# Expert tiles in two groups, each with its own plan, and the last units' chain inside the tile loops

## The chip, the cores and the metric

One core of a Trainium2 chip runs the whole program. The metric is the time of one execution on the device in microseconds (us). The engines are PE (matrix products), DVE (vector), ACT (activations), POOL (general purpose) and SP (which only issues transfers here); each runs its own instruction stream in order and waits for the others by semaphores. All data are float32, except for some masks.

## The reference

The input x is 2 x 2048 tokens of 128 features. Two layers follow one another:

```
h = norm(x) * gamma + beta;  u, z = in_proj(h)
u = silu(causal_conv4(u) + b);  dt, Bm, Cm = x_proj(u)
delta = softplus(dt_proj(dt) + b)
state = exp(delta * A) * state + delta * Bm * u      # per channel (256) and n (16), along the tokens
y = (sum_n(state * Cm) + u * D) * silu(z)
x = layernorm(x + out_proj(y) + x)

scores = softmax(x @ Wg + bg)                        # 8 experts
p, e = top_k(scores, 2)
eo[i] = gelu(x @ W1[i] + b1[i]) @ W2[i] + b2[i]      # 128 -> 512 -> 128
x = layernorm(x + p[0] * eo[e[0]] + p[1] * eo[e[1]])
```

## The kernel before

**Units and hosts.** The tokens are cut into 8 units of 512, u % 2 being the batch row. The state recurrence is a scan along the tokens: `host(j)` on each engine is the loop over unit j's 32 scans (8 quads Q of 4 scans, slot g). DVE multiplies the inflow of a quad (L1365) and runs the four scans (L1382), ACT makes the decays, PE spreads delta and adds the states up (L807), and POOL multiplies the scanned states by C in two operations per quad (`times_c`, L553, "slot"). Between them stand the front of unit j+2 and the back of units j-1 and j-2: output projection (L821), residual (L1396), norm, transpose (L830), logits (L837), the two best experts (`best_two`, `one_hots`, L1424, L1430), ranks (`ranks`: a count on PE, L851 and L853, and an addition on DVE), and places.

**Lists.** Each token goes to two experts. `run` holds the next free row of each expert's region in the DRAM tensor `xs`; `place` turns ranks into row numbers; POOL's `list_rows` (L596) writes 128 rows with an indirect transfer, 8 of them per unit, 64 in all. Behind each expert's last row SP writes 128 filler rows (`tail`, L453).

**The plan.** When all units are ranked, 14 dependent DVE steps (L1513 to L1528) turn the counts into tables: for tile n, up to MAXT = 8192 / 128 + 7 = 71, which expert (`etab`) and which rows (`rtab`). The semaphore `s_plan` counts the steps.

**The tile loops.** Tile n is 128 rows of one expert. SP loads W1 of its expert (L459, ring of 4) and its rows (L465, ring of 8, three ahead). In iteration n PE transposes tile n (`x_T`, L981), makes the hidden product of tile n-1 (L988) and the output product of tile n-2 (L996). DVE copies tile n's transpose (`x_evac`, L1533), works out the row facts of tile n-1 (L1539 to L1547), and finishes tile n-2 (`finish_tile`: bias L1553, probability L1557, row L1560). ACT makes the GELU (L1266). POOL scatters the finished tile into `results` (`scatter`, L673). The end adds the two results of each token and norms them.

**Order around the change.** After `host(7)` each engine first runs the back of units 6 and 7 and only then its tile loop. It is written out by hand: POOL lists unit 6's eight groups of rows, then unit 7's, and nothing of the tile loops starts before `s_plan` is 14 and all 64 listings have landed.

Of the kernel before, what the change touches and what calls it, by code (L numbers as in the profile page):

```python
# [12 lines left out]
P = 128  # L13
# [3 lines left out]
T = 512  # L17
# [11 lines left out]
MAXT = 2 * NTOK // P + E - 1  # L29
ROOM = NTOK // P  # L30
REGION = ROOM + 1
ROWS = 2 * NTOK + 2 * E * P
WIDE = 132

K_PARTS = {"base": E, "thresholds": ROOM, "numbers": MAXT, "lane": E, "one8": E, "idc": TT, "spare": 2 * E, "fold": 4 * 32}
# [37 lines left out]
def mamba_moe(nc, consts, bcsel, du_d, xs, results, x, ln_gamma, ln_beta, in_proj_w, conv_w, conv_b, x_proj_w,  # L73
              dt_proj_w, dt_proj_b, A_log, Dskip, out_proj_w, Wg, bg, W1, b1, W2, b2, out):
    with ExitStack() as ctx:
# [44 lines left out]
        base, thresholds, numbers, lane = const("base"), const("thresholds"), const("numbers"), const("lane")  # L120
# [77 lines left out]
        past = du[:].rearrange("p h t -> p (h t)")[:, 0:MAXT * E].rearrange("p (j e) -> p j e", e=E)  # L198
        pastc = delta[0][:].rearrange("p h t -> p (h t)")[:, 0:MAXT * E].rearrange("p (j e) -> p j e", e=E)
# [20 lines left out]
        tail = sb("tail", [P, E], U32)  # L220
# [18 lines left out]
        xT_bank, h_bank, o_bank = bank[0:2], bank[2:4], bank[5:7]  # L239
# [115 lines left out]
        def _(sp):  # L355
# [67 lines left out]
            def host(j):  # L423
# [15 lines left out]
                if j == 1:  # L439
                    sp.wait_ge(s_idle, 4)  # L440
                    sp.dma_start(xs[bass.ds(E * REGION * P, E * P), :].rearrange("(a p) w -> p a w", p=P), fillb[:])\
                        .then_inc(s_fill, 16)
# [8 lines left out]
            for e in range(E):  # L451
                r = index(tail[0:1, e:e + 1], mybir.EngineType.SP, (E * REGION - 1) * P)
                sp.dma_start(xs[bass.ds(r, P), :], fills[:, e, :]).then_inc(s_tail, 16)  # L453
            sp.wait_ge(s_plan, 14)
# [6 lines left out]
            def load_tile(n):  # L461
                r = index(rtab[0:1, n:n + 1], mybir.EngineType.SP, E * REGION + E - 1)
# [6 lines left out]
            sp.wait_ge(s_fill, 16)  # L469
            sp.wait_ge(s_tail, 16 * E)  # L470
            for b in range(B):
                sp.wait_ge(s_scat[b], 128 * (UNITS // 2))
# [1165 lines left out]
```

## Time and profile before

| | us |
|---|---|
| median of 3 timed runs | 786.08 (785.85 to 788.13) |
| profiled execution, whole | 791.61 |
| its span, first to last instruction | 789.9 |
| busy: PE, DVE, ACT, POOL | 592.4, 670.4, 428.5, 562.2 |

The profile is one execution. Times in it are microseconds from the start of the span. An entry of the timeline is a start, a duration, the engine, the line of the kernel, the operation, what it writes and reads, and in brackets how long the engine was idle before it and what it waited for.

### The profile page before, as it was taken

Reading aid. Unit: us, or ns where it says so; the run is one execution under the profiler, and the core shown is the slowest. Engines: PE = TensorE matmul, PEld = TensorE weight load, DVE = VectorE, ACT = ScalarE, POOL = GpSimd, SP = SyncE. Lnnn points to the kernel's source line nnn. Section 1 sums busy time; section 2 is a strip of 40 time slices with the busy share of each in tenths; the row PEclk is TensorE's granted clock in tenths of the full one; section 3 lists DMA queues with packets and bytes.
Section 4 is the critical chain, followed back from the end, with each engine's and each line's share of the span. In section 5 each row is a group of like instructions: output and inputs, shape, how many; then the busy total and the mean of one; then the engine's idle time right before and its main releaser. Section 6 shows DMA issues by size and latency. Waiting matters only on the chain. (4 is left out here: it accounts for less than half of the span.)

```text
span 789.9 us, 11864 instructions
## 1 busy us (share of the span) xinstructions
PE 592.4 (75%) x3055; PEld 290.2 (37%) x3071; DVE 670.4 (85%) x1349; ACT 428.5 (54%) x886; POOL 562.2 (71%) x538
## 2 busy tenths in 40 slices
PE   9768788887887888788788674676440999998920
PEld 4322222222322222222222121211130899998910
DVE  4287999999999999999998999999823688887855
ACT  3858586577467476657746554334110565555515
POOL 3345877776899799889879788878865356665634
PEclk9899999999999999999999788878755999999975
DMA  3095476566579568647556654864003677776644
GB/s 93 17 224 133 101 172 154 120 160 161 133 163 258 130 160 191 141 119 186 136 132 152 144 124 104 200 158 109 28 28 102 169 201 215 209 211 176 194 167 169
DMA packets 51169, 117.34 MB, mean 149 GB/s; under 512 B 8816, under 2 KB 25008, under 8 KB 43040
## 3 DMA queue, kind: packets, MB, share of 16 engines
q1 hardware_dynamic: 45344, 107.20, 55.7%
q0 software_dynamic: 4320, 8.99, 3.5%
q8 instruction: 26, 0.43, 0.2%
q10 hardware_dynamic: 1440, 0.40, 0.2%
q14 instruction: 39, 0.32, 0.1%
HBM read 100.21 MB, written 16.35 MB: 148 GB/s over the span
## 5 line engine op out<-in xcount | busy, mean ns | idle before, releaser
L553 POOL TENSOR_TENSOR hc<-hs,Crep 128x1024 f32<-128x1024 f32 x128 | 301.0, 2357 | 96.1 <-DVE hs L1382 85.8
L1382 DVE TENSOR_TENSOR_SCAN hs<-bank,state,flow 128x512 f32<-128x512 f32 x256 | 312.9, 1267 | 17.8 <-ACT bank L1125 11.6
L1125 ACT ACTIVATE bank<-bank,negA 128x512 f32<-128x512 f32 x256 | 164.1, 659 | 186.2 <-PE bank L798 182.6
L798 PE MATMUL bank<-delta,sel 64*128 64x512 f32 x512 | 156.7, 691 | 96.6 <-DVE hs L1382 96.2
L1365 DVE TENSOR_TENSOR flow<-flow,bank 128x2048 f32<-128x2048 f32 x63 | 142.9, 2268 | 0.0
L1266 ACT ACTIVATE flow<-bank,b1T 128x128 f32<-128x128 f32 x284 | 80.8, 369 | 57.1 <-PE bank L988 28.7
L798 PEld LDWEIGHTS bank<-delta,sel 64*128 64x128 f32 x512 | 41.8, 198 | 188.7 <-DVE hs L1382 163.6
L673 POOL DMA_INDIRECT results<-flow,idn x71 | 69.8, 983 | 33.1 <-issue 31.3
L807 PE MATMUL bank<-hc,kc 128*32 128x512 f32 x512 | 73.2, 647 | 7.8 <-POOL hc L553 7.8
L996 PE MATMUL bank<-w_sb,flow 128*128 x568 | 75.5, 276 | 4.5 <-ACT flow L1266 3.3
L988 PE MATMUL bank<-flow 128*128 128x128 f32 x568 | 76.8, 279 | 0.0
L596 POOL DMA_INDIRECT xs<-xn,pos x64 | 63.8, 998 | 16.0 <-issue 15.6
L996 PEld LDWEIGHTS bank<-w_sb,flow 128*128 128x128 f32 x568 | 69.1, 192 | 5.3 <-issue 5.2
L988 PEld LDWEIGHTS bank<-flow 128*128 128x128 f32 x568 | 70.2, 195 | 0.6 <-issue 0.2
L735 PE MATMUL bank<-hT,wtapT 128*128 128x512 f32 x128 | 64.4, 618 | 3.5 <-ACT hT L1033 1.5
L843 PE MATMUL bank<-idle_rhs,ones 128*128 128x512 bf16 x115 | 29.9, 380 | 11.4 <-DVE res L1396 6.9
L672 POOL TENSOR_TENSOR carrier<-kc 128x1 f32<-128x1 f32 x71 | 13.1, 185 | 34.5 <-DVE flow L1560 22.3
L1533 DVE COPY flow<-bank 128x128 f32<-128x128 f32 x71 | 20.7, 292 | 19.6 <-PE bank L981 13.0
L735 PEld LDWEIGHTS bank<-hT,wtapT 128*128 128x128 f32 x128 | 21.2, 189 | 40.8 <-issue 33.0
L981 PE MATMUL bank<-ident,xg 128*128 128x128 f32 x71 | 19.9, 281 | 18.2 <-DMA xg<-xs 18.2
L1553 DVE TENSOR_TENSOR flow<-bank,b_rep 128x128 f32<-128x128 f32 x71 | 20.7, 291 | 12.2 <-PE bank L996 5.9
L807 PEld LDWEIGHTS bank<-hc,kc 128*32 128x32 f32 x512 | 10.5, 111 | 53.9 <-issue 38.4
(196 smaller groups left out, 793.3 us busy)
## 6 DMA issues: line engine op xcount, KB each, us to landing
flow<-du_d SPq DMA_DIRECT2D x63, 1024.0 KB
flow<-L_ffn_W SPq DMA_DIRECT2D x71, 256.0 KB
xg<-xs SPq DMA_DIRECT2D x71, 66.0 KB
du_d<-du SPq DMA_DIRECT2D x28, 128.0 KB
xin<-L_attn_x SPq DMA_DIRECT2D x8, 256.0 KB, 3.6
hs<-results SPq DMA_DIRECT2D x8, 256.0 KB, 4.7
out<-hc SPq DMA_DIRECT2D x8, 256.0 KB, 2.0
results<-flow,idn POOLq DMA_INDIRECT x71
```

Of the source, the lines that this page charges most:

```text
L553: nc.gpsimd.tensor_tensor(hc[:, Q % 2, two, :], hs[:, Q % 2, two, :], Crep[u % 3][:].unsqueeze(1).broadcast_to([P, 2, T]), ALU.mult).then_ ...
L596: nc.gpsimd.indirect_dma_start(out=xs, out_offset=bass.IndirectOffsetOnAxis(ap=pos[u % 2][:, n:n + 1], axis=0), in_=xn[u % 2][:, n % TT, : ...
L673: nc.gpsimd.indirect_dma_start(out=results, out_offset=bass.IndirectOffsetOnAxis(ap=idn[:, n % 8:n % 8 + 1], axis=0), in_=ybuf[:, n % 8, : ...
L735: ins = nc.tensor.matmul(o[:], wtapT[:, h, k, :], hT[u % 2][:, k:k + T], start=(k == 0), stop=(k == TAPS - 1))
L798: ins = nc.tensor.matmul(dbank[2 * odd + i][:], sel[rows, odd, q % 4, :], delta[u % 2][rows, q // 4, :])
L807: ins = nc.tensor.matmul(ybank[32 * j:32 * j + 32, :], fold[:, q % 4, :], hc[:, Q % 2, j, :], start=(q % 4 == 0), stop=(q % 4 == 3))
L988: ins = nc.tensor.matmul(h_bank[n % 2][:, P * k:P * k + P], w1r[n % 4][:, P * k:P * k + P], xTs[:, n % 2, :])
L996: ins = nc.tensor.matmul(o_bank[n % 2][:, 0:D], hTs[:, n % 2, k, :], w2_sb[:].rearrange("p e k d -> p (e k d)")[:, bass.ds(e * (HK * D) + ...
L1125: nc.scalar.activation(dbank[G % 4][:], dbank[G % 4][:], ACT.Exp, scale=negA[:, ch:ch + 1]).then_inc(s_ex, 1)
L1266: ins = nc.scalar.activation(hTs[:, n % 2, k, :], h_bank[n % 2][:, P * k:P * k + P], ACT.Gelu, bias=b1T[:, bass.ds(e * HK + k, 1)])
L1365: nc.vector.tensor_tensor(flow[Q % 3][:], flow[Q % 3][:], Brep[:].unsqueeze(1).broadcast_to([P, 4, T]), ALU.mult).then_inc(s_bu, 1)
L1382: nc.vector.tensor_tensor_scan(hs[:, Q % 2, j, :], dbank[G % 4][:], flow[Q % 3][:, j, :], state[:, Q // QUADS % 2, Q % QUADS, j:j + 1], AL ...
```

## The change

The tiles are planned in two groups. Group 0 holds the rows of units 0 to 5, at most 48 + 7 = 55 tiles; group 1 those of units 6 and 7, at most 16 + 7 = 23. MAXT becomes 78. `xs` is twice as large, with a region for each expert and group; the filler rows are written once per group, those of group 1 by ACT. DVE makes the first plan in `host(7)`, one step behind each scan of slots 8 to 22, and a 15th step sets `run` to the regions of group 1. The second plan is one step per tile in iterations 24 to 37. The back of units 6 and 7 is spread over the iterations of the tile loops by a function `back_of_last(n)` on PE, ACT and DVE, and by conditions on n on POOL. Since the loops now run beside that work, their buffers are taken from other tensors, and x_T has one PSUM bank instead of two. SP waits for the rows of group 1 before it loads tile 55.

```diff
-MAXT = 2 * NTOK // P + E - 1
+GROUP_UNITS = (6, 2)
+GROUP_TILES = [2 * T * n // P + E - 1 for n in GROUP_UNITS]
+GROUP_AT = (0, GROUP_TILES[0])
+MAXT = sum(GROUP_TILES)
 ROOM = NTOK // P
 REGION = ROOM + 1
+GROUP_ROWS = (E * REGION + E) * P
+PLANNED = (14, 29)
...
-        w1r = [flow[0][:, r, :] for r in range(4)]
+        w1r = [pre[:, r, :] for r in range(4)]
         xg = sb("xg", [P, 8, WIDE])
-        xTs = flow[1][:, 2, 0:2 * P].rearrange("p (a d) -> p a d", a=2)
-        hTs = flow[1][:, 0:2, :].rearrange("p a (k n) -> p a k n", k=HK)
-        ytmp = flow[1][:, 3, 0:2 * D].rearrange("p (a d) -> p a d", a=2)
-        yprob = flow[1][:, 3, 2 * D:4 * D].rearrange("p (a d) -> p a d", a=2)
-        ybuf = flow[2][:, 0:2, :].rearrange("p a (k d) -> p (a k) d", d=D)
+        xTs = hT[0][:, 0:2 * P].rearrange("p (a d) -> p a d", a=2)
+        hTs = relu[:].rearrange("p a (k n) -> p a k n", k=HK)
+        ytmp = hT[1][:, 0:2 * D].rearrange("p (a d) -> p a d", a=2)
+        yprob = hT[1][:, 2 * D:4 * D].rearrange("p (a d) -> p a d", a=2)
+        ybuf = gated[2][:, 0:2, :].rearrange("p a (k d) -> p (a k) d", d=D)
...
-        xT_bank, h_bank, o_bank = bank[0:2], bank[2:4], bank[5:7]
+        xT_bank, h_bank, o_bank = bank[0], bank[2:4], (bank[1], bank[4])
...
+                    for p in range(2):
+                        sp.dma_start(xs[bass.ds(GROUP_ROWS * p + E * REGION * P, E * P), :]
+                                     .rearrange("(a p) w -> p a w", p=P), fillb[:]).then_inc(s_fill, 16)
...
-            sp.wait_ge(s_plan, 14)
+            sp.wait_ge(s_plan, PLANNED[0])
+            sp.wait_ge(s_silu, UNITS)
...
+            def rows_ready(p):
+                sp.wait_ge(s_plan, PLANNED[p])
+                sp.wait_ge(s_fill, 32)
+                sp.wait_ge(s_tail, 16 * E * (p + 1))
+                for b in range(B):
+                    sp.wait_ge(s_scat[b], 128 * sum(GROUP_UNITS[:p + 1]) // 2)
+
+            rows_ready(0)
...
+                if n + 3 == GROUP_AT[1]:
+                    rows_ready(1)
...
+                    if slot == 15 and not late:
+                        shift_ex(j - 1)
...
+            for n in range(MAXT + 3):
+                if n == 5:
+                    mask_ranks(last - 1)
+                if n == 9:
+                    places(last - 1)
+                    tag_rows(last - 1)
+                if 10 <= n < 10 + 4 * TT and n % 2 == 0:
+                    list_rows(last - 1, (n - 10) // 2)
+                if n == 11:
+                    back_rstd(last)
+                if n == 19:
+                    shift_ex(last)
+                if n == 22:
+                    mask_ranks(last)
+                if n == 25:
+                    places(last)
+                    tag_rows(last)
+                if 26 <= n < 26 + 4 * TT and n % 2 == 0:
+                    list_rows(last, (n - 26) // 2)
+                if n >= 3:
+                    scatter(n - 3)
...
+            def back_of_last(n):
+                if n == 0:
+                    add_states(QUADS * UNITS - 2)
+                if n == 2:
+                    add_states(QUADS * UNITS - 1)
+                if n == 3:
+                    ranks(last - 1)
+                if n == 5:
+                    out_proj(last, (0, 1))
+                if n == 6:
+                    out_proj(last, (2, 3))
+                if n == 14:
+                    xn_T(last)
+                if n == 16:
+                    logits(last)
+                if n == 19:
+                    ranks(last)
...
-                after(pe, e_xe, n - 1)
-                nc.tensor.transpose(xT_bank[n % 2][:, 0:P], xg[:, n % 8, 0:D], ident[:]).then_inc(e_xT, 1)
+                after(pe, e_xe, n)
+                nc.tensor.transpose(xT_bank[:, 0:P], xg[:, n % 8, 0:D], ident[:]).then_inc(e_xT, 1)
...
+            def fill_tail(e):
+                act.wait_ge(s_plan, PLANNED[0] + 2)
+                r = index(tail[1][0:1, e:e + 1], mybir.EngineType.Activation, 2 * GROUP_ROWS - P)
+                act.dma_start(xs[bass.ds(r, P), :], fills[:, e, :]).then_inc(s_tail, 16)
+
+            def back_of_last(n):
+                if n == 13:
+                    xns(last)
+                if n == 15:
+                    xnT_evac(last)
+                if n == 20:
+                    gate_exp(last)
+                if 27 <= n < 27 + E:
+                    fill_tail(n - 27)
...
+            def plan(p, step):
+                at, many = GROUP_AT[p], GROUP_TILES[p]
+                mine = slice(at, at + many)
+                past = past_room[:, 0:many * E].rearrange("p (j e) -> p j e", e=E)
+                pastc = pastc_room[:, 0:many * E].rearrange("p (j e) -> p j e", e=E)
+                cums = cum[:].unsqueeze(1).broadcast_to([P, many, E])
+                after(dve, s_plan, (PLANNED[0] + 1) * p + step)
+                if step == 0:
+                    drained(dve, fill_of((UNITS - 3, UNITS - 1)[p], "ranks"))
+                    ins = nc.vector.tensor_copy(tail[p][:], run[:])
+                if step == 1:
+                    ins = nc.vector.tensor_tensor(count[:], run[:], (base, base2)[p], ALU.subtract)
+                if step == 2:
+                    ins = nc.vector.tensor_tensor(over, count[:].unsqueeze(2).broadcast_to([P, E, ROOM]),
+                                                  thresholds.unsqueeze(1).broadcast_to([P, E, ROOM]), ALU.is_gt)
...
+                if step == 5:
+                    ins = nc.vector.tensor_tensor(past, numbers[:, mine].unsqueeze(2).broadcast_to([P, many, E]), cums,
+                                                  ALU.is_ge)
+                if step == 6:
+                    ins = nc.vector.tensor_tensor(pastc, past, cums, ALU.mult)
...
+                if step == 10:
+                    ins = nc.vector.scalar_tensor_tensor(lrow[:, mine], region[:, mine], float(REGION), within[:, mine],
+                                                         ALU.mult, ALU.add)
...
+                if step == 14:
+                    ins = nc.vector.tensor_copy(run[:], base2)
+                ins.then_inc(s_plan, 1)
...
+                    if 8 <= g < 23 and j == UNITS - 1:
+                        plan(0, g - 8)
...
+            def back_of_last(n):
+                if n == 4:
+                    post(last, 1)
+                if n == 5:
+                    dve.wait_ge(s_plan, PLANNED[0] + 1)
+                    ranks(last - 1)
+                if n == 7:
+                    place(last - 1)
+                if n == 8:
+                    residual(last)
+                if n == 9:
+                    back_stats(last)
+                if n == 17:
+                    best_two(last)
+                if n == 18:
+                    one_hots(last)
+                if n == 20:
+                    ranks(last)
+                if n == 23:
+                    place(last)
+                if 24 <= n < 38:
+                    plan(1, n - 24)
```

In the last host DVE's stream had, from the second unit-5 count on (`rank`, `run`: the ranks; `esum` to `posf`: the places; `hs`: a scan, x4 for four of them; `flow`: an inflow):

```order
L1437 TENSOR_TENSOR rank<-bank,run 128x32
L1440 TENSOR_TENSOR run<-run,bank 128x8
L1382 SCALAR_TENSOR_TENSOR hs<-bank,state,flow 128x512
L1390 TENSOR_TENSOR yg<-bank,gated 128x512
L1365 TENSOR_TENSOR flow<-flow,bank 128x2048
L1382 SCALAR_TENSOR_TENSOR hs<-bank,state,flow 128x512 x4
L1444 TENSOR_REDUCE esum<-ex 128x4
```

The same place on DVE now (`tail`, `count` and `rest` are the plan's first three steps):

```order
L1439 TENSOR_TENSOR yg<-bank,gated 128x512
L1414 TENSOR_TENSOR flow<-flow,bank 128x2048
L1431 SCALAR_TENSOR_TENSOR hs<-bank,state,flow 128x512
L1510 CAST tail<-run 128x8
L1431 SCALAR_TENSOR_TENSOR hs<-bank,state,flow 128x512
L1512 TENSOR_TENSOR count<-run,kc 128x8
L1431 SCALAR_TENSOR_TENSOR hs<-bank,state,flow 128x512
L1514 TENSOR_TENSOR rest<-count,kc 128x256
L1431 SCALAR_TENSOR_TENSOR hs<-bank,state,flow 128x512
L1493 TENSOR_REDUCE esum<-ex 128x4
```

A step of the plan now stands between any two of these scans. On PE the tile loop began, behind the whole chain of units 6 and 7, of which the last two counts stand here (`taken`), with the first two transposes (`ident,xg`):

```order
L853 MATMUL bank<-taken,below 128x8
L851 MATMUL bank<-taken,ones 128x8 x4
L83 TENSOR_LOAD etab
L981 MATMUL bank<-ident,xg 128x128
L83 TENSOR_LOAD etab
L981 MATMUL bank<-ident,xg 128x128
L988 MATMUL bank<-flow 128x128 x4
```

On PE it now begins right behind the host's last addition of states (`hc,kc`), and the two additions that are left stand in iterations 0 and 2:

```order
L825 MATMUL bank<-hc,kc 32x512 x4
L88 TENSOR_LOAD etab
L1010 MATMUL bank<-ident,xg 128x128
L825 MATMUL bank<-hc,kc 32x512 x4
L88 TENSOR_LOAD etab
L1010 MATMUL bank<-ident,xg 128x128
L1017 MATMUL bank<-hT,pre 128x128 x4
L88 TENSOR_LOAD etab
L1010 MATMUL bank<-ident,xg 128x128
L1017 MATMUL bank<-hT,pre 128x128 x4
```

The second addition follows the first tile's output product. On ACT, in iteration 20, the exponential of unit 7's gate now stands between two tiles' GELUs, with a table load on each side:

```order
L1311 ACTIVATE relu<-bank,b1T 128x128
L1178 ACT_TABLE_LOAD
L1178 ACTIVATE ex<-ex 128x32
L88 TENSOR_LOAD etab
L1311 ISA
L1311 ACT_TABLE_LOAD
L1311 ACTIVATE relu<-bank,b1T 128x128
```

Before, that exponential stood ahead of all GELUs, and a single table load between them.

## Rows read from the trace of the kernel before

**Rows 1.** The span in 40 slices, busy tenths of DVE.

```profile
DVE  4287999999999999999998999999823688887855
```

**Rows 2.** The chain of waits in the hole: start, us, what.

```profile
610.57 1.79 DMA xg<-xs
```

**Rows 3.** Timeline: last listings of units 5 and 7, first tile's transpose.

```profile
569.79 0.96 POOL L596 DMA_INDIRECT xs<-xn,pos  x1 [0.30 <-issue]
...
606.88 0.96 POOL L596 DMA_INDIRECT xs<-xn,pos  x1 [0.31 <-issue]
...
611.61 0.47 PE L981 MATMUL bank<-ident,xg 128*128 128x128 f32 x1 [17.90 <-DMA xg<-xs]
```

**Rows 4.** Timeline of one tile in the expert stage, DVE and PE.

```profile
645.18 0.29 DVE L1533 COPY flow<-bank 128x128 f32<-128x128 f32 x1
...
645.67 0.27 PE L981 MATMUL bank<-ident,xg 128*128 128x128 f32 x1
...
645.98 0.29 DVE L1553 TENSOR_TENSOR flow<-bank,b_rep 128x128 f32<-128x128 f32 x1
...
647.06 0.29 DVE L1533 COPY flow<-bank 128x128 f32<-128x128 f32 x1
...
647.57 0.27 PE L981 MATMUL bank<-ident,xg 128*128 128x128 f32 x1
```

**Rows 5.** Timeline, DVE in a tile in which it runs behind.

```profile
724.40 0.29 DVE L1533 COPY flow<-bank 128x128 f32<-128x128 f32 x1 [0.33 <-issue]
...
725.05 0.28 DVE L1553 TENSOR_TENSOR flow<-bank,b_rep 128x128 f32<-128x128 f32 x1
```

**Rows 6.** Timeline of host 7: scans on DVE, multiplications by C on POOL.

```profile
546.14 4.81 DVE L1382 TENSOR_TENSOR_SCAN hs<-bank,state,flow 128x512 f32<-128x512 f32 x4
...
548.67 4.73 POOL L553 TENSOR_TENSOR hc<-hs,Crep 128x1024 f32<-128x1024 f32 x2 [1.58 <-DVE hs L1382]
...
550.87 0.67 DVE L1390 TENSOR_TENSOR yg<-bank,gated 128x512 f32<-128x512 f32 x1
...
556.36 2.34 POOL L553 TENSOR_TENSOR hc<-hs,Crep 128x1024 f32<-128x1024 f32 x1 [0.27 <-DVE hs L1382]
```

**Rows 7.** Busy time by stretch (PE, PEld, DVE, ACT, POOL): chain, plan; a step.

```profile
573.00:594.60 21.60, 9.60 (x64) 7.09 (x64) 5.74 (x35) 2.69 (x7) 12.40 (x26) 0.58 0.08 26
594.60:600.85 6.25, 0.00 (x0) 0.00 (x0) 5.75 (x15) 0.00 (x0) 4.92 (x10) 0.50 0.22 67
...
596.18 0.75 DVE L1520 TENSOR_TENSOR du<-kc,cum 128x568 f32<-128x568 f32 x1
```

**Rows 8.** Timeline: two DVE operations that overlap a POOL multiplication.

```profile
440.59 3.04 DVE L1430 TENSOR_TENSOR taken<-oh 128x32 bf16<-128x32 f32 x1
441.22 2.35 POOL L553 TENSOR_TENSOR hc<-hs,Crep 128x1024 f32<-128x1024 f32 x1
...
506.18 2.36 POOL L553 TENSOR_TENSOR hc<-hs,Crep 128x1024 f32<-128x1024 f32 x1
507.83 0.80 DVE L1424 TENSOR_TENSOR oh<-kc,topi 128x64 f32<-128x64 f32 x1
```

**Rows 9.** Timeline, PE: one addition of states.

```profile
552.06 1.07 PE L807 MATMUL bank<-hc,kc 128*32 128x512 f32 x8
```

**Rows 10.** Timeline, ACT: the table load, and a GELU later in the loop.

```profile
614.70 1.28 ACT L1266 ACT_TABLE_LOAD   x1 [22.24 <-PE bank L988]
615.99 2.17 ACT L1266 ACTIVATE flow<-bank,b1T 128x128 f32<-128x128 f32 x8
...
646.97 1.14 ACT L1266 ACTIVATE flow<-bank,b1T 128x128 f32<-128x128 f32 x4 [0.76 <-issue]
648.57 1.06 PE L996 MATMUL bank<-w_sb,flow 128*128 x8
```

**Rows 11.** Timeline, POOL: scatters that find their tile finished.

```profile
717.40 0.98 POOL L673 DMA_INDIRECT results<-flow,idn  x1 [0.16 <-issue]
...
718.78 0.98 POOL L673 DMA_INDIRECT results<-flow,idn  x1 [0.16 <-issue]
```

More of the change, by code:

```diff
@@ L118, in const @@
             return kc[:, K_AT[name][0]:K_AT[name][1]]
[L120 removed]
+        base, base2, thresholds, numbers, lane = (const(n) for n in ("base", "base2", "thresholds", "numbers", "lane"))
         one8, idc, spare = const("one8"), const("idc"), const("spare")
@@ L219, in mamba_moe @@
         prob = sb("prob", [P, 8])
-        tail = sb("tail", [P, E], U32)
+        tail = [sb(f"tail{p}", [P, E], U32) for p in range(2)]
         fillb = sb("fillb", [P, E, WIDE])
@@ L651, in _ @@
                 host(j)
-            last = UNITS - 1
-            shift_ex(last - 1)
-            mask_ranks(last - 1)
-            places(last - 1)
-            tag_rows(last - 1)
-            for n in range(TT):
-                list_rows(last - 1, n)
-            back_rstd(last)
-            for n in range(TT, 2 * TT):
-                list_rows(last - 1, n)
-            shift_ex(last)
-            mask_ranks(last)
-            places(last)
-            tag_rows(last)
-            for n in range(2 * TT):
-                list_rows(last, n)
             def scatter(n):
@@ L675, in scatter @@
                     in_=ybuf[:, n % 8, :], in_offset=None).then_inc(e_sc[n % 8], 16)
-            for n in range(MAXT):
-                scatter(n)
+            last = UNITS - 1
+            for n in range(MAXT + 3):
[19 more added lines that the diff above has]
+                    scatter(n - 3)
             for u in range(UNITS):
@@ L1450, in place @@
                 nc.vector.reduce_sum(posf[:], masked[:].rearrange("p k t e -> p (k t) e"), AX_X).then_inc(s_pf, 1)
+            def plan(p, step):
[13 more added lines that the diff above has]
+                                                  thresholds.unsqueeze(1).broadcast_to([P, E, ROOM]), ALU.is_gt)
+                if step == 3:
+                    ins = nc.vector.reduce_sum(tiles[:], over, AX_X)
+                if step == 4:
+                    ins = nc.vector.tensor_tensor_scan(cum[:], one8, tiles[:], 0.0, ALU.mult, ALU.add)
+                if step == 5:
[3 more added lines that the diff above has]
+                    ins = nc.vector.tensor_tensor(pastc, past, cums, ALU.mult)
+                if step == 7:
+                    ins = nc.vector.reduce_sum(region[:, mine], past, AX_X)
+                if step == 8:
+                    ins = nc.vector.reduce_max(first[:, mine], pastc, AX_X)
+                if step == 9:
+                    ins = nc.vector.tensor_tensor(within[:, mine], numbers[:, mine], first[:, mine], ALU.subtract)
+                if step == 10:
+                    ins = nc.vector.scalar_tensor_tensor(lrow[:, mine], region[:, mine], float(REGION), within[:, mine],
+                                                         ALU.mult, ALU.add)
+                if step == 11:
+                    ins = nc.vector.tensor_scalar(expert[:, mine], region[:, mine], float(E - 1), None, ALU.min)
+                if step == 12:
+                    ins = nc.vector.tensor_scalar(rtab[:, mine], lrow[:, mine], float(GROUP_ROWS // P * p), None, ALU.add)
+                if step == 13:
+                    ins = nc.vector.tensor_copy(etab[:, mine], expert[:, mine])
+                if step == 14:
+                    ins = nc.vector.tensor_copy(run[:], base2)
+                ins.then_inc(s_plan, 1)
```

84 lines of the change are left out of this document (25 added, 59 removed).

## The prediction

> **What bounds the kernel now.** I read first the span in slices [rows 1]: DVE is at nine tenths until slice 27, falls to 2 and 3 in slices 28 to 30, and is at eight or so from there on. So there are a scan stage that DVE bounds, a hole, and an expert stage. The chain of waits has at the hole's end the wait for a tile's rows, which were just written [rows 2]. The timeline gives its edges, with POOL's listings of rows ahead of that wait [rows 3]: the last listing of unit 5 starts at 569.79, the last one of unit 7 at 606.88, and the first tile's transpose follows that by 4.73 us, at 611.61. In the expert stage PE's transposes come every 1.90 us (645.67, 647.57) and DVE's copies as well (645.18, 647.06) [rows 4]. Both engines are on the path there: PE is never idle, and DVE's whole idle time in a tile is the 0.16 us by which the step from its copy to the bias addition (0.80 in [rows 4]) exceeds that of a tile in which DVE ran behind (0.65, [rows 5]).
>
> The sum is made against the profiled execution (span 789.9, time 791.61). The median of the timed runs is 786.08, so 5.5 lower; I carry a difference over unchanged.
>
> **The start moves forward: -37.1.** The first group needs the rows of units 0 to 5 only. With the same 4.73 us behind the listing at 569.79 its first transpose would start at 574.5 instead of 611.6 [rows 3]. The W1 loads and the fills of the first group stand behind the host's last transfers on SP and are issued before that. The second filler transfer of 528 KB on SP in host 1 has three flow buffers ahead of it as cover, so I take it at nothing; uncovered it would delay a scan quad by a few us once.
>
> **The first plan goes into the last host: +8.8.** DVE gets 15 steps there, one behind each scan from the 9th to the 23rd, and host 7 runs at DVE's pace up to there: POOL waits 1.58 us for a scan at 548.67. From that point to the end of the host POOL is the late one (it waits 0.27 once more, at 556.36) [rows 6], so what DVE loses before 550 shifts the listings one for one. The 14 steps took 5.75 us of DVE time for 71 tiles [rows 7]. Four of them have 568 elements and take 0.75; with 440 they save 0.15 each, and a small copy is added: 5.3. Behind a scan an operation starts some 0.08 before its end (546.14 + 4.81 against 550.87 [rows 6]), which takes off 1.1: **4.2**.
>
> To this come collisions with POOL. At 507.83 a DVE operation on two SBUF operands that takes 0.2 alone lasted 0.80 and ended 0.09 behind POOL's multiplication [rows 8]. POOL's multiplication of 2.35 us starts some 0.1 behind the second scan of four (546.14 + 2.4, 548.67 [rows 6]). So a step behind the third scan, 1.2 us later, finds it running for another 1.15. Steps 2, 6, 10 and 14 stand there: 4 x 1.15 = **4.6**. Bounds: 4.2 if none is held, 13.6 for the rival below. I take 8.8, since each overlap in [rows 8] cost DVE the whole remainder.
>
> The Trainium skill (SBUF — State Buffer, Who interferes with whom) says that of a DVE operation with two SBUF inputs and a GpSimd operation that reads SBUF the one that issues first keeps the shared port for its whole length. By that rule the steps behind a second scan, which DVE issues just ahead of POOL, would be free, as the sum has them. A row disagrees: at 440.59 DVE was 0.63 ahead of POOL's multiplication and still ended behind it, after 3.04 us [rows 8]. There POOL had the operation queued right behind a listing; in host 7 it waits idle for the scan, so I keep these steps free and leave the row to a rival.
>
> **Seven tiles more: +13.3.** 55 + 23 = 78 tiles instead of 71, each 1.90: 7 x 1.90 [rows 4].
>
> **The chain on PE: +6.2.** It stands behind the tiles' products on an engine without idle time, so it counts in full. Two additions of states at 1.07 [rows 9] are 2.1. Output projection (two groups of 8 matmul records), logits (one) and the transpose (half a group) go at the loop's pace for such a group, (1.90 - 0.1) / 2 = 0.9: 3.2. The two rank products are some 0.45 each: 0.9. Bounds: 5.0 if the first addition falls into the wait for the first copy, 7.5 if the early ones run at the slow clock. That x_T has one bank instead of two adds nothing that the following product would not wait for anyway: both wait for the same copy.
>
> **The chain on DVE: +6.0.** Its operations of the last two units took 5.74 us in the hole [rows 7], at nine tiles of the loop. Each tile hides 0.16, and in tile 5 PE has work of its own: 5.7 - 1.4 - 0.3, and 0.5 for waits between dependent steps, makes 4.5. The second plan has 184 elements where there were 568, 3.7 us in all; over 14 tiles 2.2 of it is hidden: 1.5. Upper bound, nothing hidden: 9.6; lower bound 4.5.
>
> **On ACT: +1.6.** The exponential in tile 20 stands between GELUs: two table loads of 1.28 and 0.23. ACT is idle 0.76 in a tile, and PE needs its result only 0.46 later [rows 10]: 2.8 - 1.2 = 1.6. The normalization of 1.65 in tile 13 exceeds this by 0.4, which PE's transpose in tile 14 covers. The eight tail transfers from ACT fit in the idle 0.76; without that cover some 0.3 each, 2.4 in all.
>
> The Trainium skill (ScalarE: Activation LUTs, What ACT_TABLE_LOAD costs) gives a switch 1.28 us and 1.38 more for a drain. By that page the sum would be 2.8 higher. The trace does not agree: the load at 614.70 ends at 615.98 and the GELU starts at 615.99 [rows 10].
>
> **On POOL: +1.0.** From tile 5 to 42 it gets 16 listings at 1.27 (0.96 and 0.31 of issue, 606.88) and some 7 us of small work: 27. A scatter that finds its tile done takes 1.38 instead of 1.90 (717.40 to 718.78) [rows 3, 11], so 37 tiles give 19 back, and eight buffers allow a lag of about five tiles (9.5) more. It just fits; 1.0 is for collisions. Queued behind POOL's waits for ranks and places are the scatters, and DVE's row indices wait for scatters eight tiles back: 0 to 6.
>
> **Sum:** -37.1 + 8.8 + 13.3 + 6.2 + 6.0 + 1.6 + 1.0 = -0.2. Span 789.7, median **785.9**. The hole is really emptied, and nearly all of it is paid back in three places.
>
> **Rivals.** (B) *The plan steps aren't held by POOL.* For it: most additions of the logarithm in earlier hosts ran beside a free port. Against it: [rows 8]. Then -4.6: 781.3.
> (C) *Slower: DVE loses the port also behind the second scan.* For it: 440.59 [rows 8]. Steps 1, 5, 9 and 13 then wait 2.35 each and those behind them go free: 9.4 - 4.6 = +4.8, 790.7. It decides as soon as two of the four are held.
> (D) *DVE's idle time in the loop can't be used*, since PE takes up its copy almost at once; every operation of the chain counts in full: +3.6, 789.5. For it: only 0.22 lie between the copy's end (647.35) and PE's next transpose (647.57) [rows 4].
> (E) *The change doesn't do what it says: the second group isn't ready.* SP asks for it at tile 52, which it reaches when PE is at tile 49; POOL's last listing stands at its tile 40. With a lag over eight tiles the loop stops there: +10 or more, 796. Against it: a lag of five tiles already stops DVE.
>
> **How the numbers follow.** Forecast 0.43, B 0.27, C 0.14, D 0.11, E 0.05. What a measurement tells from no change is 0.3%, 2.4 us: below 783.7, above 788.4. The forecast's own range is 781.5 to 791 by the bounds of its terms, of which 0.12 lies below and 0.10 above that band; B gives 0.24 to faster, C, D and E 0.26 to slower. Faster 0.36, same 0.28, slower 0.36. The likeliest single case is a difference too small to see. The range 779 to 794 takes in B, C and D and leaves out E and the sums of several bounds.
>
> **What would show it.** The first tile's transpose at 583 (574.5 + 8.8); at 578 B is right, at 588 C. The 15 plan steps in host 7: those behind third scans at 1.3 us and more, the others at 0.2 to 0.6. A tile period of 1.90 outside tiles 0 to 38, and some 14 us more than that within them. The GELU of tile 20 late by 2.8. No wait of PE for rows at tile 55. I am wrong if the clock granted to PE falls in the loop, or if POOL's lag reaches the eight buffers, which would show as DVE waiting for scatters.

## The result and the profile after

The changed kernel took 814.34 us (median of 4 runs, 812.32 to 816.34), the kernel before 786.51 beside it: a ratio of 1.035 (95% interval 1.031 to 1.039), 28 us slower. The prediction was 785.9 with a range to 794. The profiled execution after has a span of 810.2 (time 812.32), 20.3 more than the 789.9 of before. The two profiled executions differ by less than the medians do, since that of before is 5.1 above its median and that of after 2.0 below; the balance below is one of 20.3 us.

The start moved as far forward as the change meant. POOL's last listing of unit 5 and the first tile's transpose, in the timeline after (columns as in [rows 3]):

```profile
572.44 0.96 POOL L609 DMA_INDIRECT xs<-xn,pos  x1 [0.30 <-issue]
577.16 0.47 PE L1010 MATMUL bank<-ident,xg 128*128 128x128 f32 x1 [11.53 <-DMA xg<-xs]
```

The transpose follows the listing by 4.72 us, as in [rows 3], and comes 34.45 earlier than the 611.61 of before. What was gained is lost in the tiles in which the last units' chain runs. Busy time of stretches after (length; PE, PEld, DVE, ACT, POOL; granted clock, DMA share, GB/s): first transpose to that of tile 5, to that of tile 42, to that of tile 55, to the last product.

```profile
577.16:590.62 13.46, 12.48 (x91) 9.44 (x92) 5.10 (x27) 5.20 (x16) 1.56 (x4) 0.78 0.47 124
590.62:698.86 108.24, 86.03 (x674) 82.05 (x672) 68.03 (x343) 47.02 (x159) 64.91 (x113) 0.94 0.54 152
698.86:724.64 25.78, 25.53 (x221) 25.17 (x222) 22.03 (x107) 14.68 (x53) 14.55 (x25) 1.00 0.66 185
724.64:777.64 53.00, 50.31 (x417) 49.00 (x415) 41.32 (x196) 28.00 (x99) 29.96 (x52) 0.97 0.61 170
```

The same stretches of the kernel before (tiles 5, 42 and 55 there too):

```profile
611.61:622.06 10.45, 8.79 (x62) 8.31 (x63) 4.86 (x26) 5.20 (x16) 1.36 (x3) 0.83 0.53 132
622.06:693.25 71.19, 70.84 (x631) 70.32 (x630) 61.60 (x298) 42.14 (x150) 43.15 (x74) 1.00 0.75 208
693.25:718.36 25.11, 25.09 (x223) 24.82 (x222) 21.37 (x103) 14.23 (x51) 15.01 (x25) 1.00 0.74 209
718.36:755.22 36.86, 34.08 (x298) 33.24 (x296) 29.61 (x143) 20.53 (x72) 21.23 (x39) 1.00 0.56 163
```

So the balance of the two profiled executions is -34.5 (start), +3.0 (to tile 5), **+37.1 (tiles 5 to 42)**, +0.7, +16.1 (the rest, seven tiles more), -2.1 (the tail): +20.3. The prediction had some 15 where 37.1 stand. PE is busy 15 us longer there (some 7 of them because it ran part of the time at half clock, see the end), but it also sits idle for 22 us, where before it was idle for 0.4. Who waited in tiles 5 to 42, first after, then before (engine and line, for whom: us in all, times, longest):

```profile
ACT relu L1311 <- PE bank L1017: 28.7, 17, 4.2
DVE hT L1611 <- PE bank L1025: 21.6, 16, 4.7
```

```profile
ACT flow L1266 <- PE bank L988: 12.7, 16, 1.4
DVE flow L1553 <- PE bank L996: 0.7, 1, 0.7
```

DVE waits for PE's products, and PE is idle: one of the two rows must be more than it seems. The timeline of such a place:

```profile
654.32 1.10 PE L1017 MATMUL bank<-hT,pre 128*128 128x128 f32 x8
654.47 0.99 POOL L609 DMA_INDIRECT xs<-xn,pos  x1 [0.16 <-issue]
655.25 1.06 PE L1025 MATMUL bank<-w_sb,relu 128*128 x8
655.86 0.99 POOL L671 DMA_INDIRECT results<-gated,idn  x1 [0.16 <-issue]
657.24 0.99 POOL L671 DMA_INDIRECT results<-gated,idn  x1 [0.16 <-issue]
658.53 0.96 POOL L609 DMA_INDIRECT xs<-xn,pos  x1 [0.30 <-issue]
658.94 1.14 ACT L1311 ACTIVATE relu<-bank,b1T 128x128 f32<-128x128 f32 x4 [4.18 <-PE bank L1017]
660.47 0.29 DVE L1611 TENSOR_TENSOR hT<-bank,b_rep 128x128 f32<-128x128 f32 x1 [3.22 <-remote]
```

PE's first product of tile 26 ends at 655.42, and ACT, idle, starts its GELU at 658.94, 3.5 us late. The second product of tile 25 ends at 656.31, and DVE adds the bias at 660.47, 4.2 us late. In the kernel before 108 of the 111 steps of this kind in tiles 5 to 42 follow within 0.2 of their data and of the engine's previous operation. So PE's work was done and what came late was the news of it. Between the two stand POOL's indirect transfers, 1.3 to 1.4 us apart with nothing but a 0.2 us operation between them. In tiles 5 to 42 of the changed kernel twenty-four steps of ACT and DVE start over 0.35 us behind both their data and their engine (43 us in all, some of it side by side), nearly all beside such a run of POOL's. The kernel before has two there, of 1.4 us together, and in its whole loop one place where a step is over 1 us late, at tiles 52 and 53. [rows 11] are its POOL side, and ACT and DVE there are these:

```profile
717.47 1.06 PE L996 MATMUL bank<-w_sb,flow 128*128 x8
720.49 1.14 ACT L1266 ACTIVATE flow<-bank,b1T 128x128 f32<-128x128 f32 x4 [3.48 <-remote]
720.60 0.29 DVE L1553 TENSOR_TENSOR flow<-bank,b_rep 128x128 f32<-128x128 f32 x1 [1.56 <-remote]
```

I had seen this stall in the trace of before and had not asked what it was.

### The profile page after: what moved, and what is told of

It reads as the page before. It is cut to its first block and busy times, and to the rows that moved or that the text cites. A ratio compares the mean times of both kernels' runs of the same rounds, so it can differ in the third digit from the quotient of the medians.

```text
span 810.2 us, 12477 instructions
## 1 busy us (share of the span) xinstructions
PE 622.7 (77%) x3190; PEld 312.2 (39%) x3190; DVE 682.7 (84%) x1420; ACT 438.9 (54%) x916; POOL 571.7 (71%) x552
## 5 line engine op out<-in xcount | busy, mean ns | idle before, releaser
L1311 ACT ACTIVATE relu<-bank,b1T 128x128 f32<-128x128 f32 x312 | 88.8, 369 | 99.7 <-PE bank L1017 41.3
L671 POOL DMA_INDIRECT results<-gated,idn x78 | 77.2, 990 | 31.7 <-issue 28.4
L1025 PE MATMUL bank<-w_sb,relu 128*128 x624 | 87.0, 285 | 10.5 <-ACT relu L1311 7.2
L1017 PE MATMUL bank<-hT,pre 128*128 128x128 f32 x624 | 90.3, 291 | 0.0
L1025 PEld LDWEIGHTS bank<-w_sb,relu 128*128 128x128 f32 x624 | 79.7, 200 | 12.0 <-issue 12.0
L1017 PEld LDWEIGHTS bank<-hT,pre 128*128 128x128 f32 x624 | 81.3, 203 | 0.3
L1611 DVE TENSOR_TENSOR hT<-bank,b_rep 128x128 f32<-128x128 f32 x78 | 22.6, 290 | 46.9 <-PE bank L1025 31.6
L1010 PE MATMUL bank<-ident,xg 128*128 128x128 f32 x78 | 23.4, 300 | 26.8 <-DVE hT L1591 13.0
L1591 DVE COPY hT<-bank 128x128 f32<-128x128 f32 x78 | 22.7, 291 | 15.7 <-PE bank L1010 9.3
L1618 DVE SCALAR_TENSOR_TENSOR gated<-xg,is_first,hT 128x128 f32<-128x128 f32 x78 | 27.5, 353 | 2.9 <-DVE hT L1615 0.2
```

What stands on the lines that cost most here:

```text
L671: nc.gpsimd.indirect_dma_start(out=results, out_offset=bass.IndirectOffsetOnAxis(ap=idn[:, n % 8:n % 8 + 1], axis=0), in_=ybuf[:, n % 8, : ...
L1017: ins = nc.tensor.matmul(h_bank[n % 2][:, P * k:P * k + P], w1r[n % 4][:, P * k:P * k + P], xTs[:, n % 2, :])
L1025: ins = nc.tensor.matmul(o_bank[n % 2][:, 0:D], hTs[:, n % 2, k, :], w2_sb[:].rearrange("p e k d -> p (e k d)")[:, bass.ds(e * (HK * D) + ...
L1311: ins = nc.scalar.activation(hTs[:, n % 2, k, :], h_bank[n % 2][:, P * k:P * k + P], ACT.Gelu, bias=b1T[:, bass.ds(e * HK + k, 1)])
```

## The experiments

**Theory R:** a run of indirect transfers on POOL without a pause holds PE's signals up. **Rivals:** L, the chain's added work on PE, DVE and ACT is what costs; P, POOL's backlog as such.

### Runs alone, without the chain

The edit to the kernel before, in POOL's loop over the tiles (2 in place of 3 for the pairs):

```
             for n in range(MAXT):
+                if n % 3 == 0:
+                    pool.wait_ge(e_ob, min(n + 3, MAXT))
                 scatter(n)
```

> The kernel before; POOL scatters the results of its 71 expert tiles in threes: it waits until the third tile of each three is finished and then issues the three scatters one right behind the other (1.38 us apart). No work is added; the result buffers are eight. In the trace of before, POOL issued three scatters in a row once (716.02, 717.40, 718.78), and there PE's products ended at 717.63 and 718.52 while ACT and DVE, which waited for them, went on at 720.49 and 720.60. Theory R (a run of three indirect transfers on POOL without a pause holds up PE's signals by about 2 us): 23 runs, each costs 2 us, +46 us, 833, and ACT's and DVE's waits for PE in nearly every third tile. Rival theory L (what slows the changed kernel's loop is the added work on PE, DVE and ACT, and the runs are only a sign of it): 786 to 788, no such waits.

> As before_in_threes, but the scatters are issued in twos. Theory R in its narrow form (only the third in a row holds PE's signals up): no loss, 786 to 789. In a wide form (every transfer that follows another without a pause costs its share): 35 pairs at 1 us, +35 us. Theory L: 786 to 788.

Threes: 828.0, ratio 1.050 (1.044 to 1.057). Pairs: 803.7, ratio 1.019 (1.013 to 1.024). One three in the timeline of before_in_threes:

```profile
641.48 0.99 POOL L673 DMA_INDIRECT results<-flow,idn  x1 [0.15 <-issue]
642.64 1.06 PE L998 MATMUL bank<-w_sb,flow 128*128 x8
642.90 1.05 POOL L673 DMA_INDIRECT results<-flow,idn  x1 [0.15 <-issue]
643.64 1.06 PE L990 MATMUL bank<-flow 128*128 128x128 f32 x8
643.67 1.14 ACT L1268 ACTIVATE flow<-bank,b1T 128x128 f32<-128x128 f32 x4 [1.48 <-PE bank L990]
644.34 0.99 POOL L673 DMA_INDIRECT results<-flow,idn  x1 [0.16 <-issue]
644.96 1.15 PE L998 MATMUL bank<-w_sb,flow 128*128 x8 [0.25 <-issue]
646.00 0.29 DVE L1555 TENSOR_TENSOR flow<-bank,b_rep 128x128 f32<-128x128 f32 x1 [2.10 <-remote]
646.11 1.14 ACT L1268 ACTIVATE flow<-bank,b1T 128x128 f32<-128x128 f32 x4 [1.29 <-PE bank L998]
```

PE's products end at 643.70 and 644.70; DVE and ACT go on at 646.00 and 646.11, 0.7 behind the end of the third transfer (645.33). In the same run of transfers PE takes up ACT's result at once: the GELU ends at 644.81 and PE's product starts at 644.96. It is news from PE that is late, not news to PE. The threes come 7.65 us apart instead of 5.7: 1.95 lost in nearly each, no work added. A pair costs about 0.6 (4.43 for two tiles instead of 3.79), between the narrow and the wide form of the expectation. L does not move here.

### Is it the missing pause, or the holding back?

The edit to before_in_threes, behind each scatter (four rows of the buffer for 05):

```
+                pool.wait_ge(s_idle, 4 + n)
+                nc.gpsimd.memset(fillb[:, 0:1], 0.0).then_inc(s_idle, 1)
```

> before_in_threes (828: ACT and DVE wait for PE in every third tile, 1.95 us lost in each) with a POOL memset of 132 elements (0.2 us) behind each scatter, so that the scatters of a three start some 1.7 us apart instead of 1.38. If what holds PE's signals up is that one indirect transfer is issued right behind another, a pause of 0.2 to 0.3 us should let most of the signals through: 786 to 800. If the holding back of three results as such costs the time (their late scatter, or three at once on the DMA queues), it stays at 825 to 835.

> As threes_pause_02 with a memset of 528 elements (0.54 us): the scatters of a three 2.0 us apart, POOL is then busy for all of a three's 5.7 us. If the missing pause holds PE's signals: none late, 786 to 792, unless POOL becomes the bound (3 x 2.1 = 6.3 us a three: +14, 800). If holding back as such: 825 to 840.

797.6 (ratio 1.012, 1.003 to 1.021, from two runs that lie 9 us apart) and 791.7 (1.004, 1.000 to 1.008), both as R has it. With transfers 1.53 to 1.6 apart a three costs about 0.5 (11 us by 23); at 1.87 apart (655.50, 657.37, 659.25) nothing is late, although POOL is now never idle:

```profile
657.37 0.99 POOL L673 DMA_INDIRECT results<-flow,idn  x1 [0.16 <-issue]
658.36 0.57 POOL L683 MEMSET fillb<- 128x528 f32 x1
658.86 1.14 ACT L1271 ACTIVATE flow<-bank,b1T 128x128 f32<-128x128 f32 x4 [0.76 <-PE bank L993]
```

### Sixteen more transfers, and nothing else

```
+AGAIN = list(range(7, 39, 2))
...
             for n in range(MAXT):
+                if n in AGAIN:
...
+                    nc.gpsimd.indirect_dma_start(
+                        out=again, out_offset=bass.IndirectOffsetOnAxis(ap=idn[:, (n - 1) % 8:(n - 1) % 8 + 1], axis=0),
+                        in_=ybuf[:, (n - 1) % 8, :], in_offset=None).then_inc(e_again, 16)
                 scatter(n)
```

> The kernel before, with 16 more indirect transfers on POOL in its expert loop: behind the scatters of tiles 6, 8, ... 36 the same rows are sent once more, to a buffer that nobody reads. That is POOL's pattern of the changed kernel (two scatters and a listing in two tiles) with none of the chain's work on PE, DVE and ACT and with neither plan nor groups moved. Theory R (runs without a pause hold PE's signals up): two tiles then ask 4.04 us of POOL where the loop has 3.8, POOL falls behind and stays in runs: 13 to 16 late signals at 1.95 us, +25 to +31 us, 812 to 818. Theory L (the chain's work is what costs): +1 to +4 us, 788 to 791.

819.7, ratio 1.040 (1.038 to 1.043). Its tiles 5 to 42:

```profile
617.64:721.23 103.59, 79.97 (x632) 75.76 (x630) 62.56 (x299) 42.59 (x151) 60.03 (x91) 0.95 0.55 156
```

103.6 instead of 71.2: +32.4, of the 37.1 that the changed kernel loses there, without chain or plan. The clock falls here too (0.95). The sixteen transfers both follow others without a pause and write to memory; this kernel doesn't tell which part of a transfer does the harm.

### The chain, without the runs

```
+NO_SCATTER = range(6, 42, 2)
...
-                if n >= 3:
+                if n - 3 in NO_SCATTER:
...
+                    nc.gpsimd.memset(fillb[:], 0.0).then_inc(s_idle, 1)
+                elif n >= 3:
                     scatter(n - 3)
```

> The changed kernel; in its tiles 6 to 40 every second scatter is left out (18 in all), and POOL clears a buffer of 1056 elements instead, which takes 0.98 us as the scatter does. So that no row of the results is undefined, SP writes zeros to them in hosts 3 to 6 (4 MB, eight transfers). POOL is as busy as in the changed kernel, PE, DVE and ACT have the same work in the loop, but POOL never has three indirect transfers in a row there. Theory R (such runs hold PE's signals up, 1.95 us each by before_in_threes): the late signals go, about 13 waits with some 27 us on the path and the spells at half clock behind them: tile 42's transpose comes 25 to 30 us earlier against tile 5's than in the changed kernel (108.2 us there, so 80), and the time is 784 to 792 if the zeros cost nothing. Theory L (added work of the chain) and P (POOL's backlog): 100 us or more from tile 5 to 42 and 808 to 816.

790.4, ratio 1.006 (1.003 to 1.009) instead of 1.035. Tiles 5 to 42, and who waited:

```profile
590.40:676.97 86.57, 79.09 (x673) 75.60 (x672) 69.03 (x344) 46.26 (x156) 64.28 (x114) 1.00 0.64 175
```

```profile
DVE hT L1630 <- PE bank L1044: 7.9, 14, 1.6
```

POOL is busy 64.3 us as in the changed kernel (64.9), and 21.7 of the 37.1 us are gone; DVE's waits for PE fall from 21.6 to 7.9, the steps that start over 0.35 us late from twenty-four (43 us) to eleven (10 us), and the granted clock is 1.00. That excludes P as the main cause, and leaves the chain at most 15.4 us: a run of three scatters remains at the start of the stretch (594.82 to 598.59) and pairs remain behind it. It also shows that the two costs don't add (32.4 + 15.4 is more than 37.1): part of the chain's work ran while PE stood idle for a late signal.

### What does a run meet in the loop?

In the hole of before, listings follow each other without a pause as well, and nothing is late: the transposes of PE that end at 588.63 are taken up at 588.66. I took transfers and then register loads out of before_in_threes. The edits: SP's `load_w1(n)` only for n = 3; then also `load_tile` only for the first eight tiles; and, separately, `chosen[n] = n % E` on PE, then on DVE and ACT too.

> before_in_threes (828) without 67 of the 71 loads of expert weights (W1, 256 KB a tile on SP's queue): each tile uses the weights that lie in its buffer. PE's work is the same. In the hole of the kernel before, listings on POOL follow each other without a pause too (585.88 to 590.76), and there ACT takes up PE's transposes at 588.66, 0.03 behind their end: no delay. What the loop has and the hole has not is SP's traffic. Theory R1 (POOL's run delays PE's signals only beside SP's large transfers, which saturate the DMA engines): 786 to 795. Theory R2 (POOL's run alone is enough as soon as PE works through it): 820 to 830, each three 1.9 us as before.

> As threes_no_w1, and without the loads of a tile's rows from tile 8 on (the first eight tiles' rows are used over and over; zeros are written to the results in hosts 3 to 6 so that none is undefined). SP sends nothing in the loop from tile 8 on. R1, or a theory R3 (it is SP's issuing of any transfer beside POOL's that counts): 786 to 795. R2: 820 to 830.

> before_in_threes (828) with PE taking tile n's expert as n modulo 8, a constant, instead of loading its number into a register for each tile (the second products use other weights than they should; the work is the same). Theory R4 (the signals wait behind PE's register load, which POOL's run holds up; in the hole PE loads no registers): the late signals go, 786 to 795. Theory R2 (no such load is needed): 820 to 832.

> As threes_pe_fixed, and DVE and ACT too take the expert as a constant, so that only SP loads registers in the loop. Theory R4 for the engines together (their register loads beside POOL's run are what fills the way): 786 to 795. R2: 820 to 832.

831.1, 829.3, 830.9 and 822.6: none brings the signals back. In threes_no_loads SP sends nothing:

```profile
655.65 0.98 POOL L677 DMA_INDIRECT results<-flow,idn  x1 [0.16 <-issue]
655.95 1.06 PE L1002 MATMUL bank<-w_sb,flow 128*128 x8
657.40 0.29 DVE L1559 TENSOR_TENSOR flow<-bank,b_rep 128x128 f32<-128x128 f32 x1 [2.22 <-PE bank L1002]
```

So SP's traffic isn't needed, by two runs of each kernel, and register loads on PE, DVE and ACT aren't either, by one run of each. In threes_all_fixed the late starts are as long as in the others (up to 2.2), but the threes come 7.33 apart instead of 7.65; that is where its 8 us lie, and why isn't tested. Why runs in the hole delay nothing stays open; PE issues products only now and then there.

### The other terms of the sum

Two banks for the transposes from tile 8 on:

```
-                after(pe, e_xe, n)
+                after(pe, e_xe, n if n < 9 else n - 1)
+        def xT_of(n):
+            return ybank if n >= 8 and n % 2 else xT_bank
```

> The changed kernel; from tile 8 on the transposes of PE go to two banks in turn (the second is the one that the scans' outputs used, free by then), so that a transpose waits for the copy of the tile but one before, as in the kernel before. Undisturbed tiles of the changed kernel are 1.99 us apart (736.14 to 771.96, 18 tiles) against 1.90 before. If the one bank is the cause, they come back to 1.90: 0.08 in each of some 50 undisturbed tiles, 4 us off 814. The prediction held that it costs nothing: then 814 and 1.99 stay.

809.85, ratio 1.028 (1.023 to 1.033) against 1.035 (1.031 to 1.039): about 4.5 us by the medians, though the intervals touch. In the traces the loop, from the first transpose to the last product, takes 197.0 instead of 200.5, and undisturbed tiles are 1.90 apart again. The changed kernel first, then this one:

```profile
744.05 0.30 PE L1010 MATMUL bank<-ident,xg 128*128 128x128 f32 x1
746.04 0.27 PE L1010 MATMUL bank<-ident,xg 128*128 128x128 f32 x1
```

```profile
742.09 0.27 PE L1013 MATMUL bank<-ident,xg 128*128 128x128 f32 x1
743.99 0.27 PE L1013 MATMUL bank<-ident,xg 128*128 128x128 f32 x1
```

The first plan behind other scans (`PLAN_AT`, scans 8 to 27 without the third of each four, in place of `8 <= g < 23`):

> after_two_banks (809.9) with the first plan's 15 steps behind scans 8 to 27 of the last host except the third ones of each four, behind which four steps took 1.53, 1.57, 1.40 and 1.26 us. If they were held by POOL's multiplication, all steps take 0.14 to 0.6, the last listing of unit 5 comes 4.4 us earlier than it would and the time is 805 to 806. Rival: the host's end is POOL's (it waits for no scan from 553.65 on), later steps shift it by themselves, or the second scans are held in place of the third: 809 to 811.

813.0, ratio 1.030 (1.028 to 1.032): no gain. Two steps, not four, are held now, and longer:

```profile
526.74 2.38 DVE L1518 TENSOR_TENSOR rest<-count,kc 128x256 f32<-128x256 f32 x1
555.37 1.99 DVE L1539 TENSOR_SCALAR expert<-region 128x55 f32<-128x55 f32 x1
```

Their excess of 3.8 is hardly less than the 4.4 of the four, and the host's last scan starts 0.8 earlier (574.57 and 575.38). A step misses one multiplication and meets another.

The marks of the chosen experts in the kernel before (`one_hots` cut in two, behind g == 1 and g == 3 instead of g == 0):

> The kernel before, with the two operations that mark the chosen experts moved in hosts 2 to 7 from behind the first scan to behind the second and the fourth. In the trace of before one of them waited 2.84 us for POOL at 440.59 and others 0.4 to 0.6 at 242.6, 374.5 and 507.8; the changed kernel's trace has no such wait at 439.54 and gained 4.3 us there by chance of timing. If those are port collisions that a place just ahead of POOL's multiplication avoids: 3 to 4 us less than before, 782 to 784. If DVE loses the port there too (the prediction's rival C): 790 or more.

812.6, ratio 1.029 (1.027 to 1.031), 23 us slower, and so the expectation was wrong in sign:

```profile
243.82 6.95 POOL L553 TENSOR_TENSOR hc<-hs,Crep 128x1024 f32<-128x1024 f32 x3
244.38 6.45 DVE L1432 TENSOR_TENSOR taken<-oh 128x32 bf16<-128x32 f32 x1
```

An addition of 0.19 us takes 6.45: it starts during POOL's first of three multiplications that follow each other, and is let through only when POOL pauses. Four waits like it and one of 4.2 in other hosts' places make 29 us more than the operations need.

### Could the change win with its transfers spaced out?

> after_two_banks (809.9) with a POOL memset of 132 elements (0.23 us) in each of POOL's turns 8 to 45, behind the scatter. Theory R: scatters 1.6 us apart instead of 1.38 let more signals through (in threes_pause_02 a three cost 0.4 us instead of 1.95), but POOL then needs 2 x 1.65 + 1.27 = 4.6 us for two tiles, 2.3 a tile, where 2.5 were taken: between 797 and 806. If signals aren't helped by pauses, POOL is only slower: 812 to 820.

813.0, ratio 1.031 (1.029 to 1.033). The pauses stood behind the scatters alone: a scatter behind a listing still began 1.36 to 1.39 after it. With a memset of 0.3 us behind each scatter and each listing:

> after_two_banks with a POOL memset of 264 elements (0.3 us) behind each listing and each scatter of the loop's turns 8 to 45; in after_paused_two_banks it stood behind the scatters alone and transfers still began 1.36 to 1.39 apart (652.07, 653.43), so that kernel didn't test what it was meant to. Now they begin some 1.65 apart. If the spacing lets signals through: late ones shrink from 1.95 to 0.4 us a run, but POOL needs 3 x 1.65 = 4.95 us for two tiles, 2.5 a tile: tile 5 to tile 42 in 92 to 100 us instead of 105.9, ratio to the kernel before 1.010 to 1.022. If it doesn't: 108 us or more and ratio 1.03 or more. Either way slower than the kernel before: POOL's 53 transfers in 37 tiles have no room.

803.0, ratio 1.017 (1.011 to 1.022). Tiles 5 to 42 in 96.65 instead of 105.92 us, at full clock:

```profile
595.44:692.09 96.65, 81.30 (x674) 75.55 (x672) 69.83 (x340) 46.03 (x155) 79.88 (x160) 1.00 0.61 168
```

The time is as expected, and still slower than before. But the late signals didn't go: twenty-seven steps start over 0.35 us late in these tiles, 37 us in all, against twenty-seven and 48 us in after_two_banks, and PE is idle for 15. Transfers 1.5 to 1.65 apart in a row that doesn't end still hold PE's signals:

```profile
664.21 1.15 PE L1040 MATMUL bank<-w_sb,relu 128*128 x8
666.14 1.00 POOL L674 DMA_INDIRECT results<-gated,idn  x1 [0.16 <-issue]
667.66 0.29 DVE L1626 TENSOR_TENSOR hT<-bank,b_rep 128x128 f32<-128x128 f32 x1 [2.33 <-remote]
```

PE's product ends at 665.36, and DVE takes it up 2.3 us later. How much of the loss left here is POOL's own pace, 4.8 us of transfers and pauses for two tiles, and how much is late signals isn't separated. Pauses as long as those of threes_pause_05 have no room here. No version here beats the kernel before.

## Why the prediction was wrong

**The start, -37.1: right.** 4.72 us behind the last listing. SP's second filler transfer cost nothing to be seen.

**The first plan, +8.8: right in size, 8.0 measured.** The last host's scans ran 5.42 us ahead of before when the plan began (511.70 against 517.12) and 2.65 behind at the end. Four steps were held for 1.0 to 1.2 each, three of them those that were named (2, 6 and 14). In the timeline after:

```profile
521.00 1.53 DVE L1514 TENSOR_TENSOR rest<-count,kc 128x256 f32<-128x256 f32 x1
530.90 1.57 DVE L1524 TENSOR_TENSOR delta<-du,cum 128x440 f32<-128x440 f32 x1
541.12 1.40 DVE L1530 TENSOR_TENSOR within<-kc,first 128x55 f32<-128x55 f32 x1
551.12 1.26 DVE L1541 COPY run<-kc 128x8 f32<-128x8 f32 x1
```

Together they took 4.4 more than they need, where the forecast had 4.6. The third row is step 9, behind a second scan, where residual and statistics of the host stand as well and push it to where POOL runs; step 10, which was named, took 0.18. So it was partly luck that the number of held steps came out as four. Rival B was wrong, and rival C was as well: the other three steps behind second scans took 0.14 to 0.6. That the transpose came at 577.2 and not at 583.3 is not B's doing: 1.1 of it is the start of the program, 0.8 the plan, and 4.3 were gained around the wait of [rows 8], at 440.59, which did not occur in this execution (0.19 at 439.54) and did in after_two_banks (3.10 at 439.01). That is luck of timing, and no part of the forecast. The runs of before scatter between 784.2 and 793.2, which would fit this one collision; it wasn't tested.

**Seven tiles more, +13.3: right** as far as it shows. From tile 55 on the kernel after takes 16.1 more, 13.3 for seven tiles, the rest mostly for the one bank.

**The one bank, "adds nothing": wrong, +4.5.** The argument was that the next product waits for the same copy anyway. It overlooked that the transpose then can't run during that wait; its 0.1 us comes behind the copy in each tile in which the copy comes just in time.

**The chain on PE, DVE and ACT, +13.8: right in size, as far as it shows.** With the runs taken away, tiles 5 to 42 cost 15.4, where the forecast has 11.7 for them (13.8 without the two additions of states, which come before tile 5). Some 2 of the 15.4 are the one bank's, by the tile periods, and an unmeasured part belongs to the late starts that were left. The ACT table loads stood where they were expected: PE waited 1.84 for the GELU behind them (639.21 to 643.33), where the forecast had 1.6.

**On POOL, +1.0: the step that failed, by more than 20.** By the forecast's own numbers POOL was asked for 37 x 1.38 + 27 = 78 us in tiles that last 70, so from tile 10 on, where two scatters and a listing ask for 2 x 1.38 + 1.27 = 4.0 us in two tiles of 3.8, its transfers had to follow each other without a gap. The step took this to cost nothing but POOL's own lateness, which eight buffers would absorb. That lateness stayed small: no scatter began more than 3.1 us behind its finished tile. What a gapless run costs instead is about 2 us of the loop on PE, an engine that shares no data with it. After each such stall POOL has caught up and waits for DVE (15 waits, 22.5 us), and then the next run builds up. Half of this was in [rows 11], 1.38 us between scatters; the stall beside them, ACT 2.9 and DVE 1.6 us behind both their data and their engines, stood in the same trace, and the forecast called PE "never idle" there.

**The clock.** I had written that I would be wrong if the granted clock fell. It did, to 0.94 over tiles 5 to 42, which is some 13 us at 1.2 GHz instead of 2.4, in four spells of 3.4 us, each behind waits of PE of about 2 us; behind the second of them ACT's table loads stood as well. The second product of tile 13 is in one:

```profile
620.76 1.92 PE L1025 MATMUL bank<-w_sb,relu 128*128 x8
```

1.92 us where 1.06 is usual. In after_memsets_2, with the same chain, the clock was 1.00 from 582 us to the loop's end, and PE was busy 79.1 us in tiles 5 to 42 instead of 86.0; the spells come with the late signals and are at most 7 us of what the runs cost. Late signals alone aren't enough for them: in before_in_threes, with a stall in nearly every three, the clock was 1.00 from 611 us to the loop's end.

**Rival E: wrong.** PE's transpose of tile 55 comes 1.98 behind that of tile 54; the second group was ready, the last listing being at 694.91. **Rival D** could not be told from the forecast: it was meant for a loss of 3.6.

## What to carry to other kernels

Before work moves onto an engine that "has idle time", ask what its idle time does for the others. Here POOL's pauses between indirect transfers let PE's signals through; two scatters per 3.8 us cost nothing, a third transfer among them costs about 2 us (32.4 us for sixteen). And a wait that a profile puts down to an engine which had long been done (PE's product ended, its reader still waits 2 us) is worth one look at what the other queues do at that time, even where it occurs once.

## What the runs showed of the hardware

- Indirect transfers that POOL issues 1.3 to 1.4 us apart hold PE's signals to ACT and DVE, while PE goes on working and takes up ACT's results without delay (644.96). The signals that become due late in a run come 0.6 to 1.1 us behind its end; in a long run some come while it lasts (658.94). Three in a row cost the loop 1.95 us, two 0.6, three at 1.53 to 1.6 us apart about 0.5, three at 1.87 apart nothing. In a row that doesn't end, 1.5 to 1.65 us apart still holds signals by up to 2.8. It needs neither SP's transfers nor register loads on PE, DVE and ACT. Which part of a transfer does it isn't tested.
- A DVE operation of 0.2 us on two SBUF operands that starts beside POOL's multiplications waits for POOL's whole row of them, 6.45 us for three. The Trainium skill (SBUF — State Buffer, Who interferes with whom) gives the port to the one that issues first, for its length. The trace agrees for the multiplication that had begun and not for the two behind it, which POOL started while DVE was waiting.
- One such collision more or less moves this kernel by some us: the same step took 3.04 at 440.59 before, 0.19 at 439.54 in the changed kernel and 3.10 at 439.01 in after_two_banks.
